# Rank part of thirteen token tiles as seven block products instead of eight, and the order of work around it

## The reference, cut to what matters

```
L0: w_eff = quantized(weight + lora_B @ lora_A * 0.5) + lora_delta ;  y = x @ w_eff.T
    logits = y @ W_router.T ; (rw, sel) = top_k(logits, 2) ; rw = softmax(rw)
    w = sum of rw * one_hot(sel)                      # per token, 8 experts
    x = x + y @ W_base.T + b_base + sum_e,r (y @ A[e,r]) * w[e] * B[e,:,r] * 2
L1: y = x @ weight.T + bias + scale * (x @ a_sel.T) @ b_sel.T   # adapter by sequence id, rank 16
    probs = softmax(y @ router_W.T) ; (tv, ti) = top_k(probs, 2) ; rw = tv / sum(tv)
    mid = (y @ lora_A) * w_dense                      # 8 experts x 16 ranks = 128 columns
    x = x + y @ base_W.T + (mid @ lora_B) * 2
```

## Time and profile before

| what | value |
|---|---|
| median of 3 runs | 908.19 us (908.16 to 908.3) |
| profiled execution, first to last instruction | 906.3 us |
| PE busy | 900.6 us, 4685 matmuls and transposes |
| DVE, ACT, POOL busy | 618.2, 311.4, 144.3 us |
| granted TensorE clock | 1.000 of full, in every slice |
| first product of tile 2 to first product of tile 15 | 432.59 to 875.53 us: 34.07 us for each of 13 tiles |

### The profile page before, as it was taken

How to read it: one execution, slowest core, us unless ns; L and a number is a source line. 1 busy time by engine, 2 the same in 40 slices (tenths; PEclk the granted TensorE clock), 3 DMA queues, 4 the chain that set the end, 5 groups by cost and what they waited for, 6 DMA issues and landing times.

```text
span 906.3 us, 13414 instructions
## 1 busy us (share of the span) xinstructions
PE 900.6 (99%) x4685; PEld 788.9 (87%) x4685; DVE 618.2 (68%) x1317; ACT 311.4 (34%) x502; POOL 144.3 (16%) x298
## 2 busy tenths in 40 slices
PE   8999999999999999999999999999999999999998
PEld 8999998888998888888888888888888888888887
DVE  6899899766587868976655655655655655656654
ACT  6588778411324334231321221221221221222220
POOL 0100000111011001414212202202202202202200
PEclk9999999999999999999999999999999999999999
DMA  9522330765412033656786886886886886886875
GB/s 360 189 96 102 118 126 24 263 199 179 140 50 94 11 128 102 222 199 236 252 288 239 294 295 236 289 295 231 291 280 250 292 295 235 286 292 238 291 258 185
DMA packets 60400, 191.45 MB, mean 211 GB/s; under 512 B 7697, under 2 KB 10666, under 8 KB 58414
## 3 DMA queue, kind: packets, MB, share of 16 engines
q1 hardware_dynamic: 49612, 158.99, 49.0%
q0 software_dynamic: 10432, 31.35, 11.7%
q10 hardware_dynamic: 290, 0.26, 0.1%
HBM read 158.86 MB, written 32.23 MB: 211 GB/s over the span
## 4 chain that ended last, share of the span: by engine, by line
PE 97%; DMA 1%; DVE 1%; ACT 0%; issue 0%; SPq 0%; DVEq 0%
PE bank L865 30%; PE bank L525 15%; PE bank L526 15%; PE bank L527 15%; PE bank L848 5%; PE bank L839 4%; PE bank L672 2%; PE bank L942 2%; PE bank L969 2%; PE bank L971 2%; PE bank L970 2%; DMA m_raw<-m1t 1%; PE bank L782 1%; PE bank L586 1%; PE bank L799 0%; PE bank L545 0%
## 5 line engine op out<-in xcount | busy, mean ns | idle before, releaser
L865 PE MATMUL bank<-g_hi,xs 128*128 128x512 f32 x448 | 145.9, 397 | 0.0
L496 POOL DMA_DIRECT2D p1sel<-p_scratch x128 | 65.3, 510 | 325.8 <-issue 325.8
L865 PE MATMUL bank<-t_hi,xs 128*128 128x512 f32 x328 | 108.3, 391 | 0.0
L865 PEld LDWEIGHTS bank<-g_hi,xs 128*128 128x128 f32 x448 | 82.2, 188 | 15.1
L998 ACT ACTIVATE xs<-x_raw 128x1024 fp32r<-128x1024 f32 x60 | 61.9, 1057 | 96.6 <-PE bank L865 95.7
L865 PE MATMUL bank<-g_lo,xs 128*128 128x512 f32 x224 | 88.8, 397 | 0.0
L1330 DVE TENSOR_TENSOR xs<-x_raw,xs 128x1024 fp32r<-128x1024 f32 x60 | 73.5, 1248 | 22.2 <-ACT xs L998 21.8
L525 PE MATMUL bank<-gx,xs 128*128 128x304 f32 x256 | 78.5, 307 | 0.0
L527 PE MATMUL bank<-gx,xs 128*128 128x304 f32 x256 | 77.4, 302 | 0.0
L526 PE MATMUL bank<-gx,xs 128*128 128x304 f32 x256 | 77.3, 302 | 0.0
L865 PEld LDWEIGHTS bank<-t_hi,xs 128*128 128x128 f32 x328 | 61.6, 188 | 12.9
(11 more groups left out here) (335 smaller groups left out, 2070.2 us busy)
## 6 DMA issues: line engine op xcount, KB each, us to landing
t_hi<-t_scratch SPq DMA_DIRECT2D x82, 512.0 KB, 5.4
t_lo<-t_scratch SPq DMA_DIRECT2D x82, 512.0 KB, 6.4
x_raw<-xq SPq DMA_DIRECT2D x16, 1024.0 KB, 9.3
out<-ost SPq DMA_DIRECT2D x62, 256.0 KB, 7.3
p1sel<-p_scratch POOLq DMA_DIRECT2D x64, 192.0 KB, 6.9
w_raw<-wall SPq DMA_DIRECT2D x16, 512.0 KB, 4.9
w<-e_scratch SPq DMA_DIRECT2D x6, 1024.0 KB, 5.1
ea<-e_scratch POOLq DMA_DIRECT2D x8, 644.0 KB, 4.3
```

Source lines behind the costliest of these rows:

```text
L496: pool.dma_start(f(p1sel[b][STK * s:STK * s + STK, cs]), p1_dram[bass.ds(i * STK, STK), cs]).then_inc(sems[b], 16)
L865: mm = nc.tensor.matmul(bk[j][:], l[:, c, :], m[:, c, :], start=first and c + k == 0, stop=c + k == KH + 1, skip_group_check=True)
```

## The change

The rank part of tiles 2 to 14 is taken as one 2x2 block product. The left side has the blocks m0 and mid for both token blocks, the right side P0 and LB1 in two column halves, and seven products take the place of eight. For that the right side's sums `k1` to `k4` are made once, during tiles 0 and 1: 9 sums and 4 low parts on DVE, 4 high parts on ACT. `k2` takes the place of P0's right half, which is stored to HBM and loaded again for the last tile, whose rank part stays as it was (4 transfers of 256 KB). The left side's sums are made per tile: `s3_sum`, `s3_low`, three sums in `rank_sums`, three low parts in `rank_low` on DVE (all 128x128), and on ACT a copy of the transposed m0 (128x256), the high part of s3 (128x128) and one of 128x384 (`srk_hi`).

On PE, `m0_terms(0)` moves into the chain behind `at_x1` and now ends with `p1_mm`; the product with s3 follows product 72; four products follow `low_terms`, then the low term of bank 3 and the last product, which waits for `x6_ok`. Two of the products go to bank 4. The second half of the next tile's narrow product now ends the tile. The chain's places move from (12, 20, 34, 44) to (20, 26, 36, 47). On DVE all output sums stand ahead of the next gate, and there are three more of 128x512 (`u3_part`, `b3`, `b1`). `p5_sum` for bank 3 waits for the s3 product. SP stores the outputs in another order. The scratch of POOL's transfers is set to 4096 bytes per partition, and some semaphores are shared.

```diff
-CHAIN = [(30, 44, 62, 76), (13, 24, 42, 56), (12, 20, 34, 44)]
+CHAIN = [(30, 44, 62, 76), (13, 24, 42, 56), (20, 26, 36, 47)]
+R7, R6, R4, R2, R3, R5, NR = 1, 2, 3, 4, 5, 6, 6
...
             load_x(1)
+            sp.wait_ge(g_lo_s, O_ALL)
+            for k, p in enumerate((p0_hi, p0_lo)):
+                sp.dma_start(p0_dram[k], f(p[:, 512:D])).then_inc(st_p0, 16)
...
-                store_out(tau, (3, 0) if tau + 1 < NT2 else (1, 0))
+                elif tau + 2 == NT2:
+                    sp.wait_ge(s_lo_s, 2 * (NT2 - REG))
+                    sp.wait_ge(st_p0, 48)
+                    for k in range(2):
+                        sp.dma_start(f(p0r[:, k, :]), p0_dram[k]).then_inc(ld_p0, 16)
+                store_out(tau, (2, 0) if tau + 1 < NT2 else (1, 0))
...
                     mm.then_inc(c_mm, 1)
+                    if REG <= tau < NT2 - 1:
+                        m0_terms(0).then_inc(p1_mm, 1)
...
-                pe.wait_ge(ev[3], tau)
+                pe.wait_ge(b3_ok if n else ev[3], n or tau)
...
                 pe.wait_ge(ev[0], tau)
-                product(12, 0, quarter(0, 0, 0), g_quarter(0, 0), True).then_inc(p1_mm, 1)
+                mm = product(12, 0, quarter(0, 0, 0), g_quarter(0, 0), True)
+                if tau + 1 == NT2:
+                    mm.then_inc(p1_mm, 1)
...
                 if tau + 1 < NT2:
                     product(72, 3, quarter(1, 1, 0), (t_hi, t_lo), False, lambda: t_loaded(1, 2)).then_inc(t_free, 1)
+                    pe.wait_ge(rs_hi_s, 2 * n + 1)
+                    pe.wait_ge(rs_lo_s, 2 * n + 1)
...
+                    rank_product(bk[3][:], (s3_hi, s3_lo), (k3_hi[:], k3_lo[:])).then_inc(rank_mm, 1)
...
+            def rank_products(tau):
...
+                pe.wait_ge(rs_hi_s, 2 * n + 2)
+                pe.wait_ge(rs_lo_s, 2 * n + 2)
...
+                rank_product(bk[4][:], s2, (k2_hi, k2_lo), True).then_inc(rank_mm, 1)
+                rank_product(bk[2][:], mid[1], (k4_hi[:], k4_lo[:])).then_inc(rank_mm, 1)
+                rank_product(bk[0][:], mid[0], lbl).then_inc(rank_mm, 1)
+                rank_product(bk[1][:], s4, lbr).then_inc(rank_mm, 1)
+                low_terms(tau, (3,))
+                pe.wait_ge(x6_ok, n + 1)
+                rank_product(bk[4][:], s1, (k1_hi[:], k1_lo[:])).then_inc(rank_mm, 1)
...
                 winograd_products(tau)
                 if tau + 1 < NT2:
-                    low_terms(tau, (0, 2, 1, 3))
+                    low_terms(tau, (0, 2, 1))
+                    mid_ready(tau)
+                    rank_products(tau)
                     x_product(tau + 1, (1,))
-                    mid_ready(tau)
-                    mid_terms()
...
             def out_copy(tau, j):
-                act.wait_ge(out_mm, tau * 4 + (3, 0, 2, 1).index(j) + 1)
+                if tau < REG:
+                    act.wait_ge(out_mm, tau * 4 + (3, 0, 2, 1).index(j) + 1)
+                else:
+                    act.wait_ge(rank_mm, NR * (tau - REG) + R2)
...
                 nc.scalar.activation(p5_sum[:], bk[3][:], ACT.Identity).then_inc(p5_ok, 1)
+                if tau + 1 < NT2:
+                    act.wait_ge(m0t_lo_s, tau + 1)
+                    nc.scalar.activation(m0, TR[:, 0:T2].rearrange("p (b n) -> p b n", b=2), ACT.Identity).then_inc(m0r_s, 1)
...
                 mid_high(tau)
                 if tau + 1 < NT2:
+                    act.wait_ge(rs_raw_s, 2 * n + 2)
+                    hi_of(srk_hi[:], srk_raw).then_inc(rs_hi_s, 1)
                     s_high(tau + 1, 1)
                     s_high(tau + 1, 0)
                     rex(tau + 1, 0)
                     out_copy(tau, 0)
...
             k_high(k4_hi[:], k4_raw[:], 4)
...
                 mid_low(tau)
                 if tau + 1 < NT2:
-                    v.wait_ge(t_free, 6 * n + 6)
+                    rank_sums(tau)
+                    rank_low(tau)
+                    v.wait_ge(rank_mm, NR * n + R7)
                     nc.vector.tensor_tensor(p5_sum[:], bk[3][:], p5_sum[:], ALU.add).then_inc(u3_ok, 1)
+                    u3_part(tau)
                     s_low(tau + 1)
-                    front(tau + 1, lambda: out_sum(tau, 1, 3, p1_sum))
-                    v.wait_ge(u3_ok, n + 1)
-                    out_sum(tau, 3, 2, p5_sum)
-                    v.wait_ge(u4_ok, n + 1)
-                    out_sum(tau, 4, 1, u4_sum)
+                    out_parts(tau)
+                    u4_part(tau)
+                    last_outs(tau)
+                    front(tau + 1)
...
-    nc = _bacc.Bacc("TRN2", target_bir_lowering=False, num_devices=1)
+    nc = _bacc.Bacc("TRN2", target_bir_lowering=False, num_devices=1, dynamic_dma_scratch_size=4096)
```

More of the change, by code:

```diff
@@ L842, in plain_products, with m0_terms, rank_product @@
                 mm.then_inc(g_all, 1)
-            def m0_terms(j, first=False, to=None):
+            def m0_terms(j, first=False, to=None, right=(p0_hi[:, 512:D], p0_lo[:, 512:D])):
                 b, h = j // 2, j % 2
-                hs = slice(h * 512, h * 512 + 512)
-                for k, (l, m) in enumerate(((m0t_hi, p0_hi), (m0t_hi, p0_lo), (m0t_lo, p0_hi))):
-                    nc.tensor.matmul(bk[j][:] if to is None else to, vt(l, b), m[:, hs], start=first and k == 0, stop=k == 2, skip_group_check=True)
+                hi, lo = right if h else (p0_hi[:, 0:512], p0_lo[:, 0:512])
+                for k, (l, m) in enumerate(((m0t_hi, hi), (m0t_hi, lo), (m0t_lo, hi))):
+                    mm = nc.tensor.matmul(bk[j][:] if to is None else to, vt(l, b), m, start=first and k == 0, stop=k == 2, skip_group_check=True)
+                return mm
+            def rank_product(dst, s, t, first=False):
+                for k, (l, m) in enumerate(((s[0], t[0]), (s[0], t[1]), (s[1], t[0]))):
+                    mm = nc.tensor.matmul(dst, l, m, start=first and k == 0, stop=k == 2, skip_group_check=True)
+                return mm
             def winograd_products(tau):
@@ L896, in winograd_products @@
                 product(36, 0, quarter(0, 0, 1), g_quarter(1, 0), False)
+                last = tau + 1 == NT2
+                p0_right = (p0r[:, 0, :], p0r[:, 1, :])
                 pe.wait_ge(ev[2], tau)
-                m0_terms(2, True)
+                if last:
+                    m0_terms(2, True)
                 t_loaded(0, 1)
-                product(48, 2, quarter(0, 1, 1), (t_hi, t_lo), False, lambda: t_loaded(1, 1)).then_inc(t_free, 1)
-                pe.wait_ge(ev[1], tau)
-                m0_terms(1, True)
-                product(60, 1, quarter(1, 0, 1), g_quarter(1, 1), False)
+                product(48, 2, quarter(0, 1, 1), (t_hi, t_lo), not last, lambda: t_loaded(1, 1)).then_inc(t_free, 1)
+                pe.wait_ge(b1_ok if n else ev[1], n or tau)
+                if last:
+                    pe.wait_ge(ld_p0, 48)
+                    m0_terms(1, True, None, p0_right)
+                product(60, 1, quarter(1, 0, 1), g_quarter(1, 1), not last)
                 mid_turn(tau)
@@ new lines, in u3_part, with out_parts @@
+            def u3_part(tau):
+                n = tau - REG
+                v.wait_ge(u3_ok, n + 1)
+                v.wait_ge(rank_mm, NR * n + R6)
+                tt(p5_sum[:], bk[4][:], p5_sum[:], ALU.add).then_inc(x6_ok, 1)
+            def out_parts(tau):
+                n = tau - REG
+                v.wait_ge(low_mm, tau + 1)
+                tt(p1_sum[:], bk[3][:], p1_sum[:], ALU.add).then_inc(b3_ok, 1)
+                v.wait_ge(rank_mm, NR * n + R4)
+                v.wait_ge(x6_ok, n + 1)
+                out_sum(tau, 2, bk[2], p5_sum)
@@ L1874, in _ @@
             t_low(2)
+            k1_sum()
             front(1)
@@ L1892, in _ @@
                 low_rank(tau)
+                if tau + 1 < NT2:
+                    s3_sum(tau)
+                if not n:
+                    v.wait_ge(k_raw_s, 4)
+                    k_low(4, k4_lo[:], k4_raw[:], k4_hi[:])
                 v.wait_ge(p5_ok, n + 1)
```

179 lines of the change are left out of this document (139 added, 40 removed).

## The result

The changed kernel takes **917.85 us** (median) where the kernel before takes 908.21: ratio 1.0133, 95% interval 1.0087 to 1.0179. It is slower by 9.6 us. Of the four executions of the changed kernel one took 927.91 us at a mean granted clock of 0.989 (the kernel before has such ones too, 919.83 at 0.989 among others); the middle one of the other three took 917.58. The forecast was 915.9, with a range of 911.5 to 921.0. The profiled execution took 917.5 us and has a span of 915.8, where 914.0 was forecast.

What follows compares the result with a forecast made beforehand. The prediction took PE as the bound, busy 900.6 of 906.3 us. Saved matmuls (-9.0) and two new waits (+12.6, +4.1) gave +7.7 us: span 914.0, median 915.9 us, range 911.5 to 921.0.

Steps and rivals of the forecast that it cites:

- What goes: PE's rank part: 28 to 25 matmuls per tile in 13 tiles, 39 fewer at 0.231 each, 9.0 us less.
- Wait A: PE's product 12 waits for ACT's copy of bank 0, resuming 0.15 later: 0.97 us, 13 times, 12.6 us.
- X: Start of the narrow product's last matmul on PE, from which times around a tile's border are counted.
- Wait B: PE's product 24 waits for ACT's copy of bank 3 behind m0t_hi: 0.29 us, 14 tiles, 4.1 us.
- The gate's end: m0 written at X + 4.77, before the transposes at X + 5.7: no cost; without Wait A, some 0.2 us.
- DVE in front of the gate: DVE's sums and low parts ahead of the gate finish in time, with 0.35 us of slack, the thinnest cover.
- The rival built on it: DVE late at the gate, sums 0.72 apart throughout: 3.3 us more, 919.2 us; chance 0.12.
- The rank sums, the setup, the stores: Rank sums ready at 525.7, needed at 527.6; setup in DVE's idle places, at most some tenths once; moved stores cost nothing.
- SP's loads: Loads of t_hi, t_lo start some 2 us later, land 6.4 us after issue; product 48 over 9 us behind: hidden.
- The sum: -9.0 + 12.6 + 4.1 = +7.7 us: span 914.0, median 915.9 us, bounds 912.7 to 917.5.
- The copy in time: Faster rival: bank 0's copy on ACT ends by X + 2.7, so Wait A goes: 905.9 us; chance 0.07.
- The clock: Rival: PE's pauses drop twelve matmuls behind Wait A to 1.2 GHz, 2.74 us more per tile, 951 us; chance 0.03.

Runs made afterwards that it cites:

- r7_chain28: Changed kernel with bank 0's copy ahead of the exponential, bank 3's ahead of m0_high on ACT, and chain places (22, 28, 36, 47): 899.47 us.
- r6_minus3: Kernel before, leaving out three rank matmuls of 512 columns per tile in tiles 2 to 14, output not the reference's: 907.23 us.
- r2_p5_first: Changed kernel with bank 3's copy to p5_sum ahead of m0_high on ACT, the exponential still ahead of bank 0's copy: 914.03 us.
- r3_both: Changed kernel with two exchanges on ACT, bank 0's copy ahead of the exponential and bank 3's copy ahead of m0_high: 902.89 us.
- r1_copy_first: Changed kernel with one exchange on ACT, bank 0's copy ahead of the next gate's exponential: 906.62 us.

## Why the prediction was right

Point by point, in its own steps.

- **What goes**, 9.0 us. Right as a size: 34.08 to 33.38 is 0.70 for three matmuls, 0.23 each, and `r7_chain28` is 8.8 below before. The rule in the Trainium skill, "TensorE: Matmul & The Clock Gate", section "Back-to-back issue gap", would give 8.4 by its 216 ns for an isolated gap, an estimate from that page; the traces stay with 0.23. What the prediction did not see is that the saving could be had only with some change of order: `r6_minus3` kept 1.1 of it.
- **Wait A**, 0.97 forecast, 0.99 measured. X + 3.70 for the copy's end was 3.71. The resumption was put at 0.15; it is 0.05 (539.38 to 539.43), and 0.11 come back in a longer step to the second matmul. That the two errors cancel is luck. The 0.15 came from a row of transposes; where transposes wait for DVE in `r6_minus3` it is 0.15 again, but a 128x512 matmul goes on sooner. (The lower bound, 0.03, is 0.04 by the rows shown: 532.22 to 532.26.)
- **Wait B**, 0.29 forecast, 0.30 measured; `r2_p5_first` gave back 3.8 us and the second edit in `r3_both` 3.7, against 4.1 forecast. The same two errors cancel here: in tile 5 the copy ends at 542.68, the matmul starts at 542.73, 0.19 late, and the next one comes 0.34 behind it.
- **The gate's end**, "some 0.2" at the transposes if wait A were gone: 0.20 in `r3_both` at that place, though only 0.10 to 0.16 of it stay in a tile's length. So `r1_copy_first` gave back 11.2 us and not the 10.3 of its expectation.
- **DVE in front of the gate**, slack 0.35 forecast, 0.16 measured (the row at 536.01). Of the five sums one started 0.77 behind the one before it (533.79 to 534.56), not 0.60. The cover that the prediction called the thinnest held, with half the margin; product 72's, below, did not. The rival built on it did not come.
- **The rank sums, the setup, the stores**: no wait of PE names them. Tile 2's product 0 starts at 432.87 instead of 432.59, and 0.26 of this stand there already at 352 us, before the setup's operations.
- **SP's loads**: here a step failed. The prediction worked out the cover for product 48 and called the loads hidden. It didn't look at product 72, whose cover loses three matmuls. It also took a median, 6.4 us, for the landing, where over all traces one in seven of the loads ahead of product 72 needed more than 7.12. It cost 1.1 us in tile 14 and about 0.3 in others of the profiled execution. The thinner cover is enough for how often such waits come; why the longest last so long stays open.
- **The sum**: forecast span 914.0, plus 0.28 at tile 2's start, 1.1 and 0.3: 915.7, and 915.8 was measured. By its own bounds the forecast was 912.7 to 917.5, and the measured 917.85 lies above them. That it lies within the stated range is owed to the room that was left for DVE being late, which did not happen. The mechanism and the size of both waits were right; that the range held was in part luck.
- **The rivals.** The copy in time would be `r1_copy_first`: it was forecast at 905.9 and measured 906.62, so the price was right to 0.7 and the condition not fulfilled. The clock: 1.00 in the stretch above, with 0.75 us of idle time in each tile. The pattern that the Trainium skill, the same page, section "A second HAM failure mode: psum-queue depth-cycling", tells of did not appear with these pauses.

## What to carry to other kernels

Where one engine is busy all the time, a saving on it shortens the time of everything that runs beside it, so ask for each wait that is covered by the removed work how much of its cover is left; here a gate had 0.1 to 0.2 us, and 9 us of saving came to 1. When work is moved to make that room, write down for each consumer the last matmul that covers it, before and after: an instruction on another engine that stands in front for no reason (a copy behind an exponential, a copy behind a high part) cost nothing here for as long as it was covered, and 11 us (the copy behind the exponential) and 3.7 us (the copy behind the high part) once it wasn't. The remedy was not to take the change back but to exchange two pairs of lines and move two numbers, 917.85 to 899.47.
